# State-space layer of a two-layer network: C products two ring places back, halos on ScalarE, another layout of a chunk's side work

## The chip, the cores and the metric

One Trainium2 chip, of which the program uses one core. The metric is device time in microseconds, the median over runs; less is better.

## The reference

A network of two layers over 2048 rows of 512 features: attention and a mixture of experts, then a selective state space (Mamba) layer and a permuted MLP, each behind a layer norm. The change is in the state-space layer, for which the reference reads, cut to what matters:

```python
proj = hidden_states @ W_in.T
u, gate = jnp.split(proj, 2, axis=-1)                 # 1024 channels each
x = conv_general_dilated(transpose(u), conv_w, padding=[(K - 1, 0)], feature_group_count=D)   # K = 4 taps
u = silu(transpose(x) + conv_b)
dt, Bm, Cm = split(u @ Wx.T, [R, R + N])              # R = 32, N = 16; each then rms-normed
delta = softplus(dt @ Wdt.T + dt_bias)
def step(state, xs):
    d_t, B_t, C_t, u_t = xs
    state = exp(d_t[..., None] * A) * state + (d_t * u_t)[..., None] * B_t[:, None, :]
    return state, einsum('bdn,bn->bd', state, C_t)
y = (scan(step) + u * D_param) * silu(gate)
return y @ W_out.T
```

## The kernel before

The stage works on 8 chunks (c) of 256 time steps. In a chunk there are 8 tiles of 128 channels (t) and, for each, 4 groups of states (gr), so 32 units (q), numbered Q over the whole stage. A unit is a tile of 128 partitions x 4 parts (j) x 256 steps, held in `scan`, a ring of 8 places. What is done to a unit:

- the drive: `spread` multiplies the repeated delta*u (`rep`) by the B rows (`bc`), on GpSimd for even units and on VectorE for odd ones, into `drive`;
- the decays: ScalarE's `decays` writes exp(delta*A) into PSUM, four passes a unit, through three half-unit banks;
- the scan: VectorE's `unit` does four TENSOR_TENSOR_SCANs in place, and after each second unit copies the last states into `state` (the carry);
- the C product: GpSimd multiplies the scanned states by the C rows, into `read`;
- the sum: TensorE's `sum_states` adds over states, two units later (`LAG`); at the end of a channel tile the skip product, and then VectorE's `gate_y`.

`drive` and `read` are the same memory: a part has 257 columns, `drive` is columns 1 to 256 and `read` columns 0 to 255. The C product is thus written in place one column to the left, and the last column keeps the state for the carry. `bc` begins two elements (`PHASE`) off the alignment of the other tiles.

Between the units every engine does side work for the next chunk (and the output of the chunk before), at places that tables of numbers give: on TensorE `AT` says before which unit stand the projection of u (`proj`, 4 pairs of channel tiles), the convolution (`conv`), the rows of B, C and dt (`rows`, `square`, `rms`), the step sizes (`step`), the gate's projection (`gate`) and the output product (`out`) of the chunk before. On ScalarE `U_COPY`, `CONV_OUT`, `SILU`, `ROWS_OUT`, `RMS`, `GATE_OUT`, `STEP_OUT`, `GATE_SILU`, `H_OUT` (`modulate`) and `OUT_COPY` say before which unit's decays their copies and functions stand, on VectorE `NORMED` (`rms_norm`), `DELTA` (`step_sizes`) and two tables for the halos. Each of TensorE's side products takes one of two PSUM banks in turn (`PLACE`), and waits until the product two before it has been read out. The engines' queues are in order, so a late item holds up all behind it.

The halo is the last three columns of u's projection, which the convolution of the next chunk needs: VectorE copies them from `halo` into `upre` and from `upre` into `halo`, a TENSOR_REDUCE of 6 elements each, for each of the 4 pairs of a chunk.

Of the kernel before, what the change touches and what calls it, by code (L numbers as in the profile page):

```python
# [2100 lines left out]
```

## Time and profile before

| | |
|---|---|
| median of 3 runs | 1946.83 us (1944.97 to 1953.23) |
| profiled execution, its own time | 1953.82 us |
| its span, first to last instruction | 1952.0 us |
| busy in the span: TensorE, VectorE, ScalarE, GpSimd | 1620.1, 1375.3, 1094.4, 966.5 us |
| mean granted TensorE clock | 0.829 of full speed |
| state-space stage, first scan to last | 865.7 to 1825.4 us |

The busy times are over the whole program. The part that the change touches is the state-space stage, in which VectorE, GpSimd and TensorE all have much to do, and what counts there is who waits for whom, unit by unit.

### The profile page before, as it was taken

The numbers are of one execution on the slowest core, as the hardware profiler recorded it, in microseconds if no ns is written. First come the engines' busy times: TensorE is split into PE (matmuls) and PEld (weight loads), VectorE is DVE, ScalarE is ACT, GpSimd is POOL, SyncE is SP. The second block draws the span as 40 slices with busy tenths as digits, with TensorE's granted clock in tenths as the row PEclk, the third lists the DMA queues.
The fourth block names the chain that finished last, engine by engine and source line by source line (L and its number), as shares of the span: only waits on it lengthen the run. The fifth ranks groups of instructions, "written<-read, shape, count | busy, mean of one in ns | idle before, by whom it ended". The sixth has DMA issues, their size and how long they took to land. (4 is left out here: it accounts for less than half of the span.)

```text
span 1952.0 us, 24260 instructions
## 1 busy us (share of the span) xinstructions
PE 1620.1 (83%) x8168; PEld 866.7 (44%) x8168; DVE 1375.3 (70%) x2292; ACT 1094.4 (56%) x2026; POOL 966.5 (50%) x598
## 2 busy tenths in 40 slices
PE   6888999999879995778688797987979879745558
PEld 2522222222147443555366474664746647423322
DVE  3257888888064215037998899989999889999423
ACT  2333666667712013257766767668676676765227
POOL 0000000001033203437998898888988888999403
PEclk9765999999965796778699796997969979767678
DMA  5311000000083446633543445434454344645022
GB/s 225 153 53 55 3 3 3 3 3 3 6 279 147 155 135 237 215 88 80 121 112 93 103 112 126 109 92 103 117 123 108 92 104 101 133 98 124 17 92 87
DMA packets 152988, 195.78 MB, mean 100 GB/s; under 512 B 17907, under 2 KB 123139, under 8 KB 151198
## 3 DMA queue, kind: packets, MB, share of 16 engines
q1 hardware_dynamic: 143692, 167.19, 33.0%
q0 software_dynamic: 4608, 16.80, 2.4%
q10 hardware_dynamic: 4564, 10.24, 1.4%
q8 instruction: 65, 1.06, 0.2%
q14 instruction: 59, 0.48, 0.1%
HBM read 141.81 MB, written 52.37 MB: 99 GB/s over the span
## 5 line engine op out<-in xcount | busy, mean ns | idle before, releaser
L1811 DVE TENSOR_TENSOR_SCAN ssm_scan<-ssm_psum,ssm_state,ssm_scan 128x256 f32<-128x256 f32 x1024 | 680.0, 728 | 59.6 <-ACT ssm_psum L1698 59.6
L1430 POOL TENSOR_TENSOR ssm_scan<-ssm_scan,ssm_bc 128x1024 f32<-128x1024 f32 x256 | 557.4, 2181 | 117.7 <-DVE ssm_scan L1811 117.4
L1698 ACT ACTIVATE ssm_psum<-ssm_rep,ssm_a 128x256 f32<-128x256 f32 x1024 | 435.6, 467 | 193.4 <-DVE ssm_scan L1811 191.2
L641 ACT ACTIVATE att_probs<-att_psum 128x1024 f32<-128x1024 f32 x256 | 248.5, 1021 | 108.4 <-PE att_psum L577 108.2
L678 DVE TENSOR_REDUCE att_rowmax<-att_psum 128x1 f32<-128x512 f32 x448 | 278.1, 682 | 42.0 <-PE att_psum L559 42.0
L1534 PE MATMUL ssm_psum<-ssm_scan,ssm_select 128*32 128x256 f32 x2048 | 190.9, 459 | 98.7 <-POOL ssm_scan L1430 98.4
L1410 POOL TENSOR_TENSOR ssm_scan<-ssm_rep,ssm_bc 128x1024 f32<-128x1024 f32 x128 | 255.7, 1998 | 9.5 <-DMA ssm_rep<-drive_rows 9.5
L530 POOL COPY att_v<-v_tokens 128x128 f32<-128x128 f32 x8 | 2.3, 295 | 332.2 <-ACT att_out L635 332.2
L559 PE MATMUL att_psum<-att_k,att_q 72*128 72x512 bf16 x448 | 160.6, 399 | 3.7 <-DVE att_rowmax L678 2.2
L1796 DVE TENSOR_TENSOR ssm_scan<-ssm_rep,ssm_psum 128x1024 f32<-128x1024 f32 x128 | 156.1, 1220 | 1.4 <-DMA ssm_rep<-drive_rows 1.4
L1512 PE MATMUL ssm_psum<-ssm_h,late_weights 128*128 128x256 f32 x512 | 134.0, 421 | 18.2 <-DVE ssm_delta L1785 15.1
L588 PE MATMUL att_psum<-att_probs,att_v 128*32 128x512 f32 x1024 | 139.0, 615 | 0.6 <-ACT att_probs L641 0.6
L1534 PEld LDWEIGHTS ssm_psum<-ssm_scan,ssm_select 128*32 128x32 f32 x2048 | 47.0, 118 | 200.2 <-POOL ssm_scan L1430 109.7
L1478 PE MATMUL ssm_psum<-ssm_upre,late_weights 128*128 128x256 f32 x512 | 132.0, 416 | 3.5 <-ACT late_turned L1611 3.5
L577 PE MATMUL att_psum<-att_q,att_k 74*128 74x512 bf16 x448 | 132.2, 379 | 0.7 <-ACT att_probs L641 0.2
L1468 PE MATMUL ssm_psum<-ssm_h,late_weights 128*128 128x256 f32 x512 | 122.7, 395 | 7.9 <-ACT ssm_h L1593 7.0
L1512 PEld LDWEIGHTS ssm_psum<-ssm_h,late_weights 128*128 128x128 f32 x512 | 105.8, 212 | 50.5 <-DVE ssm_delta L1785 21.2
L1520 PE MATMUL ssm_psum<-ssm_gate,late_weights 128*128 128x256 f32 x512 | 121.0, 391 | 0.6 <-issue 0.6
L1478 PEld LDWEIGHTS ssm_psum<-ssm_upre,late_weights 128*128 128x128 f32 x512 | 104.2, 208 | 33.0 <-ACT late_turned L1611 6.7
L1505 PE MATMUL ssm_psum<-ssm_normed,ssm_wdt 32*128 32x256 f32 x128 | 63.8, 648 | 64.4 <-DVE ssm_delta L1785 32.3
L1468 PEld LDWEIGHTS ssm_psum<-ssm_h,late_weights 128*128 128x128 f32 x512 | 98.9, 197 | 30.7 <-issue 14.7
L1520 PEld LDWEIGHTS ssm_psum<-ssm_gate,late_weights 128*128 128x128 f32 x512 | 98.7, 196 | 20.5 <-issue 6.6
(232 smaller groups left out, 1894.0 us busy)
## 6 DMA issues: line engine op xcount, KB each, us to landing
ssm_rep<-drive_rows SPq DMA_DIRECT2D x256, 256.0 KB, 4.8
qkv_wmod<-in_wmod SPq DMA_DIRECT2D x8, 1536.0 KB, 12.0
late_weights<-in_we SPq DMA_DIRECT2D x8, 1024.0 KB, 14.4
ssm_bc<-bc_rows SPq DMA_DIRECT2D x32, 256.0 KB, 5.0
drive_rows<-ssm_delta SPq DMA_DIRECT2D x64, 128.0 KB
drive_rows<-ssm_du SPq DMA_DIRECT2D x64, 128.0 KB
sorted_rows<-moe_zeros SPq DMA_DIRECT2D x1, 5888.0 KB, 19.2
moe_sorted<-sorted_rows SPq DMA_DIRECT2D x23, 256.0 KB, 3.5
```

Of the source, the lines that this page charges most:

```text
L559: nc.tensor.matmul(ps_m[n % MB], q[0:QROWS, tile[m // QC]], k[0:QROWS, chunk[m % QC]], start=True, stop=True).then_inc(max_scored, 1)
L641: nc.scalar.activation(probs[:, u % RING, :].rearrange("p (j t) -> p j t", j=2), ps_s[u % 2], ACT.Exp).then_inc(exp_done, 1)
L678: nc.vector.tensor_reduce(rowmax[:, m:m + 1], ps_m[n % MB], AX.X, ALU.max).then_inc(max_done, 1)
L1410: nc.gpsimd.tensor_tensor(drive[:, Q % RING], rep[:, s % 2, 1], bc[:, c % 2, 0, gr, :].unsqueeze(1).to_broadcast([P, J, SW]), ALU.mult).th ...
L1430: nc.gpsimd.tensor_tensor(read[:, Q % RING], drive[:, Q % RING], bc[:, c % 2, 1, gr, :].unsqueeze(1).to_broadcast([P, J, SW]), ALU.mult).t ...
L1468: last = nc.tensor.matmul(halves("proj", c, pair)[:, i], win[:, k, m:m + P], h[:, c % 2, k, :], start=(k == 0), stop=(k == KT - 1))
L1478: last = nc.tensor.matmul(halves("conv", c, pair)[:, i], conv[:, 2 * pair + i, k, :], upre[:, pair % 2, i, k:k + SW], start=(k == 0), stop ...
L1512: last = nc.tensor.matmul(halves("gate", c, pair)[:, i], win[:, k, m:m + P], h[:, c % 2, k, :], start=(k == 0), stop=(k == KT - 1))
L1520: nc.tensor.matmul(bank("out", c, m)[:, 0:SW], wout[:, t, m * P:(m + 1) * P], gate[:, c % 2, t, :], start=(t == 0), stop=False)
L1534: last = nc.tensor.matmul(ps_y[t % 2][32 * j:32 * j + 32, :], select[:], read[:, Q % RING, j, :], start=(gr == 0), stop=False)
L1698: nc.scalar.activation(ps_decay[n % HALF_BANKS][:, i], rep[:, s % 2, 0, j, :], ACT.Exp, scale=amat[:, t, gr, j:j + 1]).then_inc(decay_done, 1)
L1811: nc.vector.tensor_tensor_scan(drive[:, Q % RING, j, :], ps_decay[(2 * Q + j // 2) % HALF_BANKS][:, j % 2], drive[:, Q % RING, j, :], stat ...
```

## The change

`scan` loses its extra column. `drive(Q)` is place Q of the ring, and `read(Q)` is place Q - 2: the C product no longer overwrites its own input but the place of the unit two before, whose carry has been taken by then. A place is used again six units after the C product was written there, so the spreads wait for a later sum. `halo` gets two copies, one for each parity of chunk, and ScalarE fills and reads it in `copy_u`; VectorE's two halo functions and their semaphores go. The tables get other numbers, `AT` holds lists, and `modulate` moves from unit 24 to unit 12.

```diff
-        halo = sb("ssm_halo", [P, DT, TAPS - 1])
+        halo = sb("ssm_halo", [P, 2, DT, TAPS - 1])
-        scan = sb("ssm_scan", [P, RING, J, SW + 1])
-        drive, read = scan[:, :, :, 1:], scan[:, :, :, 0:SW]
+        scan = sb("ssm_scan", [P, RING, J, SW])
...
-              9: ("conv", 3), 10: ("out", 0), 11: ("out", 1), 12: ("out", 2), 13: ("rows", 0), 14: ("out", 3), 15: ("square", 0),
+              10: [("conv", 3), ("out", 0)],
+              12: [("out", 1)],
+              14: [("rows", 0)],
+              17: [("square", 0), ("out", 2)],
...
-        SILU, ROWS_OUT, RMS, GATE_SILU, H_OUT = 13, 16, 18, 31, 24
+        SILU, ROWS_OUT, RMS, GATE_SILU, H_OUT = 15, 17, 19, 31, 12
...
-        OUT_COPY = {12: 0, 13: 1, 14: 2, 16: 3}
+        OUT_COPY = {14: 0, 18: 1, 19: 2, 21: 3}
+        def drive(Q):
+            return scan[:, Q % RING]
+        def read(Q):
+            return scan[:, (Q - 2) % RING]
...
-                if Q >= RING:
-                    pool.wait_ge(sum_done, Q - RING + 1)
-                    pool.wait_ge(carry_done, (Q - RING) // 2 + 1)
-                nc.gpsimd.tensor_tensor(drive[:, Q % RING], rep[:, s % 2, 1],
+                if Q >= RING - 2:
+                    pool.wait_ge(sum_done, Q - RING + 3)
+                    if Q >= RING:
+                        pool.wait_ge(carry_done, (Q - RING) // 2 + 1)
+                nc.gpsimd.tensor_tensor(drive(Q), rep[:, s % 2, 1],
...
                     pool.wait_ge(scan_done, (Q + 1) * J)
-                    nc.gpsimd.tensor_tensor(read[:, Q % RING], drive[:, Q % RING],
+                    if Q >= 2:
+                        pool.wait_ge(carry_done, Q // 2)
+                        pool.wait_ge(read_done, Q - 1)
+                    nc.gpsimd.tensor_tensor(read(Q), drive(Q),
...
-                    act.wait_ge(halo_saved, n - 1)
+                if n >= DP:
+                    act.wait_ge(upre_out, n - DP + 1)
+                pair_of = slice(2 * pair, 2 * pair + 2)
+                nc.scalar.copy(upre[:, pair % 2, :, 0:TAPS - 1], halo[:, c % 2, pair_of, :])
+                nc.scalar.copy(halo[:, (c + 1) % 2, pair_of, :], halves("proj", c, pair)[:, :, SW - TAPS + 1:])
                 nc.scalar.copy(upre[:, pair % 2, :, TAPS - 1:], halves("proj", c, pair)).then_inc(upre_out, 1)
...
-                if Q >= RING:
-                    dve.wait_ge(sum_done, Q - RING + 1)
+                if Q >= RING - 2:
+                    dve.wait_ge(sum_done, Q - RING + 3)
```

ScalarE around the silu of u (the two ACT_TABLE_LOADs with an ACTIVATE of 128x2048 between them), before, units 11 to 14 of a chunk; `ssm_psum<-ssm_rep,ssm_a` x4 are the decays of one unit, `ssm_xout` an output copy:

```order
L1611 ACTIVATE late_turned<-ssm_psum,ssm_convb 128x256 x2
L1678 COPY ssm_xout<-ssm_psum 128x256
L1698 ACTIVATE ssm_psum<-ssm_rep,ssm_a 128x256 x4
L1615 ACT_TABLE_LOAD
L1615 ACTIVATE late_turned<-late_turned 128x2048
L1588 ACT_TABLE_LOAD
L1678 COPY ssm_xout<-ssm_psum 128x256
L1698 ACTIVATE ssm_psum<-ssm_rep,ssm_a 128x256 x4
L1678 COPY ssm_xout<-ssm_psum 128x256
L1698 ACTIVATE ssm_psum<-ssm_rep,ssm_a 128x256 x8
```

and with the change, from `modulate` (128x256 x4 into `ssm_h`) before unit 12 to unit 16:

```order
L1617 ACTIVATE ssm_h<-ssm_h,mod 128x256 x4
L1726 ACTIVATE ssm_psum<-ssm_rep,ssm_a 128x256 x4
L1639 ACTIVATE late_turned<-ssm_psum,ssm_convb 128x256 x2
L1726 ACTIVATE ssm_psum<-ssm_rep,ssm_a 128x256 x4
L1706 COPY ssm_xout<-ssm_psum 128x256
L1726 ACTIVATE ssm_psum<-ssm_rep,ssm_a 128x256 x4
L1643 ACT_TABLE_LOAD
L1643 ACTIVATE late_turned<-late_turned 128x2048
L1612 ACT_TABLE_LOAD
L1726 ACTIVATE ssm_psum<-ssm_rep,ssm_a 128x256 x8
```

An output copy stood right ahead of the silu's unit and one right behind the silu; now the one ahead is a unit earlier, behind nothing but a convolution's copy, and `modulate` has come in two units before that.

ScalarE around the first step size of a chunk (`ssm_delta<-ssm_psum,ssm_dtb` is a step's first pass), before:

```order
L1698 ACTIVATE ssm_psum<-ssm_rep,ssm_a 128x256 x20
L1593 ACTIVATE ssm_h<-ssm_h,mod 128x256 x4
L1651 ACTIVATE ssm_delta<-ssm_psum,ssm_dtb 128x256 x2
L1655 ACTIVATE ssm_psum<-ssm_psum,ssm_dtb 128x256 x2
L1657 ACTIVATE ssm_psum<-ssm_psum 128x512
L1659 ACTIVATE ssm_psum<-ssm_psum 128x512
```

and with the change:

```order
L1726 ACTIVATE ssm_psum<-ssm_rep,ssm_a 128x256 x8
L1693 COPY ssm_gate<-ssm_psum 128x512
L1679 ACTIVATE ssm_delta<-ssm_psum,ssm_dtb 128x256 x2
L1683 ACTIVATE ssm_psum<-ssm_psum,ssm_dtb 128x256 x2
L1685 ACTIVATE ssm_psum<-ssm_psum 128x512
L1687 ACTIVATE ssm_psum<-ssm_psum 128x512
L1726 ACTIVATE ssm_psum<-ssm_rep,ssm_a 128x256 x4
```

`modulate` stood between 20 decays and the step; now a gate copy stands there.

TensorE from the first output product (`ssm_gate,late_weights` with `ident,ssm_xres`) on, before; `ssm_wx` is `rows`, `ssm_group` is `square`, `ssm_scan,ssm_select` x4 the sum of one unit, `ssm_skip` the skip product:

```order
L1520 MATMUL ssm_psum<-ssm_gate,late_weights 128x256 x8
L1524 MATMUL ssm_psum<-ident,ssm_xres 128x128 x2
L1534 MATMUL ssm_psum<-ssm_scan,ssm_select 32x256 x4
L1520 MATMUL ssm_psum<-ssm_gate,late_weights 128x256 x8
L1524 MATMUL ssm_psum<-ident,ssm_xres 128x128 x2
L1534 MATMUL ssm_psum<-ssm_scan,ssm_select 32x256 x4
L1520 MATMUL ssm_psum<-ssm_gate,late_weights 128x256 x8
L1524 MATMUL ssm_psum<-ident,ssm_xres 128x128 x2
L1534 MATMUL ssm_psum<-ssm_scan,ssm_select 32x256 x4
L1485 MATMUL ssm_psum<-late_turned,ssm_wx 64x256 x8
L1534 MATMUL ssm_psum<-ssm_scan,ssm_select 32x256 x4
L1539 MATMUL ssm_psum<-late_turned,ssm_skip 128x256
```

and with the change:

```order
L1509 MATMUL ssm_psum<-late_turned,ssm_wx 64x256 x8
L1558 MATMUL ssm_psum<-ssm_scan,ssm_select 32x256 x12
L1515 MATMUL ssm_psum<-ssm_group,ssm_normed 128x3 x2
L1544 MATMUL ssm_psum<-ssm_gate,late_weights 128x256 x8
L1548 MATMUL ssm_psum<-ident,ssm_xres 128x128 x2
L1558 MATMUL ssm_psum<-ssm_scan,ssm_select 32x256 x4
L1563 MATMUL ssm_psum<-late_turned,ssm_skip 128x256
L1521 MATMUL ssm_psum<-ident,ssm_rwide 64x128 x2
L1558 MATMUL ssm_psum<-ssm_scan,ssm_select 32x256 x4
L1544 MATMUL ssm_psum<-ssm_gate,late_weights 128x256 x8
L1548 MATMUL ssm_psum<-ident,ssm_xres 128x128 x2
L1536 MATMUL ssm_psum<-ssm_h,late_weights 128x256 x8
```

Before, three outputs stood ahead of `rows` with one sum between each two, and the fourth right behind; now output 2 comes after `rows`, three sums and `square`, and output 3 is followed at once by a gate product (`ssm_h,late_weights`) with no sum between.

## Rows read from the trace of the kernel before

**Rows 1.** Windows: engines' busy us (x instructions), granted clock, DMA share, GB/s.
```profile
core 0: us, PE busy (x) PEld busy (x) DVE busy (x) ACT busy (x) POOL busy (x), PEclk, DMA share, GB/s
989.00:1598.00 609.00, 521.11 (x2924) 346.50 (x2920) 553.58 (x905) 424.26 (x946) 530.09 (x280) 0.85 0.48 109
1598.00:1716.00 118.00, 98.56 (x568) 64.77 (x568) 110.47 (x182) 83.32 (x187) 104.86 (x56) 0.88 0.48 108
1716.00:1830.00 114.00, 59.44 (x370) 26.73 (x370) 109.04 (x174) 57.57 (x135) 105.59 (x55) 0.60 0.41 93
```

**Rows 2.** Timeline of VectorE: silu of u in chunk 0; unit 31 of chunks 0, 5, 6, 7.
```profile
921.05 1.39 DVE L1811 TENSOR_TENSOR_SCAN ssm_scan<-ssm_psum,ssm_state,ssm_scan 128x256 f32<-128x256 f32 x2 [1.19 <-ACT ssm_psum L1698]
...
988.82 1.39 DVE L1811 TENSOR_TENSOR_SCAN ssm_scan<-ssm_psum,ssm_state,ssm_scan 128x256 f32<-128x256 f32 x2 [2.88 <-ACT ssm_psum L1698]
...
1598.17 1.39 DVE L1811 TENSOR_TENSOR_SCAN ssm_scan<-ssm_psum,ssm_state,ssm_scan 128x256 f32<-128x256 f32 x2 [3.11 <-ACT ssm_psum L1698]
...
1715.82 1.39 DVE L1811 TENSOR_TENSOR_SCAN ssm_scan<-ssm_psum,ssm_state,ssm_scan 128x256 f32<-128x256 f32 x2 [1.47 <-ACT ssm_psum L1698]
...
1822.73 2.66 DVE L1811 TENSOR_TENSOR_SCAN ssm_scan<-ssm_psum,ssm_state,ssm_scan 128x256 f32<-128x256 f32 x4
```

**Rows 3.** Groups by line, 840 to 1860 us: busy, mean ns, idle before.
```profile
L1811 DVE TENSOR_TENSOR_SCAN ssm_scan<-ssm_psum,ssm_state,ssm_scan 128x256 f32<-128x256 f32 x1024 | 680.0, 728 | 59.6 <-ACT ssm_psum L1698 59.6
...
L1430 POOL TENSOR_TENSOR ssm_scan<-ssm_scan,ssm_bc 128x1024 f32<-128x1024 f32 x256 | 557.4, 2181 | 117.7 <-DVE ssm_scan L1811 117.4
...
L1410 POOL TENSOR_TENSOR ssm_scan<-ssm_rep,ssm_bc 128x1024 f32<-128x1024 f32 x128 | 255.7, 1998 | 9.5 <-DMA ssm_rep<-drive_rows 9.5
...
L1823 DVE TENSOR_TENSOR ssm_gate<-ssm_psum,ssm_gate 128x256 f32<-128x256 f32 x64 | 25.9, 405 | 11.1 <-PE ssm_psum L1539 11.1
...
L1678 ACT COPY ssm_xout<-ssm_psum 128x256 f32<-128x256 f32 x32 | 11.9, 372 | 73.1 <-PE ssm_psum L1524 73.0
...
L1773 DVE TENSOR_REDUCE ssm_halo<-ssm_upre 128x6 f32<-128x6 f32 x28 | 4.2, 151 | 0.3 <-DVE ssm_upre L1767 0.3
```

**Rows 4.** Timeline of VectorE, chunk 4: start, length, idle before.
```profile
1404.86 2.67 DVE L1811 TENSOR_TENSOR_SCAN ssm_scan<-ssm_psum,ssm_state,ssm_scan 128x256 f32<-128x256 f32 x4 [3.38 <-ACT ssm_psum L1698]
...
1416.98 5.24 DVE L1811 TENSOR_TENSOR_SCAN ssm_scan<-ssm_psum,ssm_state,ssm_scan 128x256 f32<-128x256 f32 x8 [0.81 <-ACT ssm_psum L1698]
...
1426.79 0.42 DVE L1823 TENSOR_TENSOR ssm_gate<-ssm_psum,ssm_gate 128x256 f32<-128x256 f32 x1 [0.62 <-PE ssm_psum L1539]
...
1445.10 0.69 DVE L1785 TENSOR_TENSOR ssm_delta<-ssm_delta,ssm_psum 128x512 f32<-128x512 f32 x1 [1.36 <-ACT ssm_psum L1659]
```

**Rows 5.** Timeline of ScalarE, chunk 4, units 12, 18 and 24.
```profile
1397.11 0.37 ACT L1678 COPY ssm_xout<-ssm_psum 128x256 f32<-128x256 f32 x1 [2.09 <-PE ssm_psum L1524]
1397.37 1.67 ACT L1698 ACTIVATE ssm_psum<-ssm_rep,ssm_a 128x256 f32<-128x256 f32 x4
1399.06 1.28 ACT L1615 ACT_TABLE_LOAD   x1
...
1403.58 0.37 ACT L1678 COPY ssm_xout<-ssm_psum 128x256 f32<-128x256 f32 x1
...
1421.81 0.50 ACT L1639 ACTIVATE ssm_rwide<-ssm_rms 128x64 f32<-128x64 f32 x3
...
1440.21 2.07 ACT L1593 ACTIVATE ssm_h<-ssm_h,mod 128x256 f32<-128x256 f32 x4
```

**Rows 6.** Timeline of TensorE, chunk 4, around units 2 and 28.
```profile
1363.19 0.64 PE L1534 MATMUL ssm_psum<-ssm_scan,ssm_select 128*32 128x256 f32 x8 [2.91 <-POOL ssm_scan L1430]
1363.76 5.41 PE L1478 MATMUL ssm_psum<-ssm_upre,late_weights 128*128 128x256 f32 x16
...
1369.67 3.72 PE L1468 MATMUL ssm_psum<-ssm_h,late_weights 128*128 128x256 f32 x16
...
1436.22 1.08 PE L1534 MATMUL ssm_psum<-ssm_scan,ssm_select 128*32 128x256 f32 x8
...
1457.63 6.25 PE L1512 MATMUL ssm_psum<-ssm_h,late_weights 128*128 128x256 f32 x16 [2.15 <-DVE ssm_delta L1785]
...
1464.38 3.72 PE L1512 MATMUL ssm_psum<-ssm_h,late_weights 128*128 128x256 f32 x16
```

**Rows 7.** Groups of GpSimd: the fold of the gate into the output weights.
```profile
L1416 POOL TENSOR_TENSOR late_weights<-late_weights,ssm_xout 128x512 f32<-128x512 f32 x8 | 9.9, 1276 | 0.0
```

More of the change, by code:

```diff
@@ L1255, in state_space @@
         xdst = scratch.x3.rearrange("(k p) t -> p k t", p=P)
-        AT = {0: ("proj", 0), 1: ("proj", 1), 3: ("conv", 0), 4: ("proj", 2), 5: ("conv", 1), 6: ("proj", 3), 7: ("conv", 2),
-              9: ("conv", 3), 10: ("out", 0), 11: ("out", 1), 12: ("out", 2), 13: ("rows", 0), 14: ("out", 3), 15: ("square", 0),
-              16: ("gate", 0), 17: ("gate", 1), 19: ("rms", 0), 21: ("step", 0), 22: ("step", 1),
-              24: ("step", 2), 25: ("step", 3), 27: ("gate", 2), 28: ("gate", 3)}
+        AT = {0: [("proj", 0), ("proj", 1)],
+              3: [("conv", 0)],
+              4: [("proj", 2)],
+              6: [("conv", 1)],
+              7: [("proj", 3)],
+              9: [("conv", 2)],
+              10: [("conv", 3), ("out", 0)],
+              12: [("out", 1)],
+              14: [("rows", 0)],
+              17: [("square", 0), ("out", 2)],
+              18: [("rms", 0)],
+              19: [("out", 3), ("gate", 0)],
+              20: [("step", 0)],
+              22: [("step", 1), ("gate", 1)],
+              23: [("step", 2)],
+              26: [("gate", 2)],
+              28: [("step", 3), ("gate", 3)]}
         AHEAD = {"proj": 1, "conv": 1, "gate": 1, "rows": 1, "square": 1, "rms": 1, "step": 1, "out": -1}
@@ L1266, in state_space @@
         LATE = {0: ("gate", 2), 1: ("step", 2), 2: ("gate", 3), 3: ("step", 3)}
+        STEP_AHEAD = (1, 1, 1, 1)
         def at(c, q):
@@ L1273, in at @@
             if q in AT:
-                kind, i = AT[q]
-                if 0 <= c + AHEAD[kind] < SCH:
-                    found.append((kind, c + AHEAD[kind], i))
+                for kind, i in AT[q]:
+                    of = c + (STEP_AHEAD[i] if kind == "step" else AHEAD[kind])
+                    if 0 <= of < SCH:
+                        found.append((kind, of, i))
             return found
@@ L1533, in sum_states @@
                 for j in range(J):
-                    last = nc.tensor.matmul(ps_y[t % 2][32 * j:32 * j + 32, :], select[:], read[:, Q % RING, j, :],
+                    last = nc.tensor.matmul(ps_y[t % 2][32 * j:32 * j + 32, :], select[:], read(Q)[:, j, :],
                                             start=(gr == 0), stop=False)
@@ L1825, in _ @@
             dve.wait_ge(zeroed, 2)
-            for pair in range(DP):
-                carry_halo(0, pair)
-                save_halo(0, pair)
             dve.wait_ge(weights_in, 16 * 8)
```

46 lines of the change are left out of this document (14 added, 32 removed).

## The prediction

> **What bounds the kernel now.** The state-space stage is about half of the span, so I read it chunk by chunk in the windows [rows 1]: over chunks 1 to 5 VectorE is busy 553.58 of 609 us, 110.7 a chunk, and idle 11.1. GpSimd (530.09, 106.0 a chunk) and TensorE (521.11, 104.2) are close behind. The last chunk has no side work; from its predecessor's last unit to its own it is 1822.73 - 1715.82 = 106.9 us [rows 2], 3.34 a unit, the floor as the scan is written. The steady period is (1598.17 - 988.82) / 5 = 121.9 [rows 2]. So 3.8 us a chunk is VectorE's side work and 11.1 is waiting.
>
> Whom it waits for is in [rows 3]: the scans for ScalarE's decays 59.6 us, the gating product for TensorE's sums 11.1. Where, is in [rows 4], chunk 4: 3.38 at unit 13, 0.81 at unit 16, 0.62 for a sum at 19, 1.36 for a step size at 24; and about 3 more at unit 31 (2.88 and 3.11 in [rows 2]). Why, is on ScalarE [rows 5]. Its decays have three half banks, so it can be at most 1.5 units ahead. Before the silu of u it waits 2.09 us for output product 0; then table load, silu and table load take 1403.58 - 1399.06 = 4.5 us, and another output copy stands before the decays of unit 13. At unit 24 the 2.07 us of `modulate` stand ahead of a step size. Two places show a silu with less in front of it [rows 2]: 1.19 us in chunk 0, which has no output copies, and 1.47 at the end of chunk 6, which has no `modulate`.
>
> **The change, part by part.** (a) *Order on ScalarE.* `modulate` goes to unit 12, and units 13 and 14 hold one small copy each. ScalarE needs 1.67 us a unit for decays [rows 5] against VectorE's 3.34, so it is 1.5 units ahead again by unit 14. The silu of u moves to unit 15; output 0 was multiplied at unit 10, so nothing is waited for, and the other output copies come after it. I price each silu at the undisturbed 1.2 us (ends: 0.7, if ScalarE starts it as early as the banks allow, and 1.5): 2.4 a chunk for two. Step sizes now stand at 23, 24, 27, 29. A step takes ScalarE about 2.8 us (its four passes stand between the end of `modulate`, two microseconds after 1440.21, and the delta at 1445.10 [rows 4, 5]). From unit 23: gate copy 0.5, step 2.8, decays 1.7, step 2.8. VectorE comes to the first delta with 0.9 to spare and to the second just as it is ready: 0.3 (ends 0 and 1.4, the wait now). Steps 2 and 3 stand behind units in which ScalarE recovers.
>
> The table switches bear on the silu's floor. The Trainium skill ("ScalarE: Activation LUTs", what a table load costs) adds a drain of about 1.38 us to each load of 1283 ns. By that the block of 4.5 us would be 7.2, each of 14 silus would cost 2.7 us more, 38 in all, and a fifth of the gain would be left. The trace shows no such drain behind the loads, so the rows decide.
>
> (b) *Order on TensorE.* Outputs 2 and 3 go from units 12 and 14 to 17 and 19, so four output products and `rows` no longer stand nearly back to back, which made the sum 0.62 late [rows 4]. New waits take their place: `rows` (unit 14) waits for the silu, 3 to 5 us of idle TensorE; `square` (17) needs the bank that output copy 1 gives back at ScalarE's unit 18; and `rms_norm` stands at unit 19, not 21. From the silu's end: `rows` 3.7, its copies 0.7, decays, the copy of output 1 and `square` 3.7, output 2 about 4.2, a sum and `rms` 1.8: 14.1 us. VectorE reaches `rms_norm` 14.0 after the silu. I take a wait of 0.5, with ends 0 and 2: after 2.91 us of idle TensorE the next 16 products took 5.41 us where 3.72 is usual [rows 6], and that may befall `rows`.
>
> (c) *The ring.* C products are written two places back, so a place is free only six units after its use, not eight: a spread of unit Q needs sum Q-6. The tightest is the spread of unit 23, which needs sum 17, queued behind output 3 and gate 0 (7.9 us at full clock). By the same walk it ends some 2 us before: no cost. With 6.25 us for 16 products, as at half clock [rows 6], it is 3 to 4 us late. The new waits of the C product, on the carry and on itself, cost nothing: both precede the scan for which GpSimd waits anyway.
>
> (d) *GpSimd's durations.* The C product takes 2181 ns, the B spread 1998 [rows 3]. Both multiply 1024 elements by the same bc tile, two elements off alignment. The spread's other input is aligned; the C product reads and writes the scan tile in runs of 257-element step. Without the column it has the spread's pattern, so I take 1998: 256 x 0.18 = 47 us less on GpSimd, none on the path, since the scans wait for ScalarE alone [rows 3]. Ends: 2181, and 2.55 us, twice the 1276 ns of a 512-element product whose three operands start alike [rows 7]. VectorE's scans already start at four different offsets in a unit, and four take 2.67 us everywhere [rows 4]; I expect no change there.
>
> (e) *Halos.* VectorE loses 2 x 28 reduces of 0.15 us [rows 3], which overlap their neighbours and cost some 0.11 each: 0.9 us a chunk. ScalarE gets two small copies before each of its `copy_u`. It has no such row; bounds are 0.17 us, a third of three passes of 32 elements or fewer [rows 5], and nothing. At most 8 x 0.17 = 1.4 us a chunk, in units 2, 3, 6 and 10, where ScalarE waits for VectorE. Before the first unit they are partly on the path: +0.7.
>
> **Sum.** A steady chunk keeps 2.4 + 0.3 + 0.5 of waits and 0.5 of gaps too small for a row, 3.7 instead of 11.1; with the halos -8.3, over five chunks -41.5. Chunk 0 keeps its late gate and step work in units 0 to 5; of 1.19, 1.4 and 2.88 later it keeps 3, and halos: -3.3. Chunk 6 has 118 - 110.5 = 7.5 us idle [rows 1]: to 3.7, and halos, -4.7. The start +0.7. Together -48.8 us. The profiled execution took 1953.82, so about 1905; it was 7 us above the median of the three runs, 1946.83, and against that I say 1898.
>
> **Rivals.** *A: TensorE's chain.* A chunk falls to about 113 us while TensorE needs 104 of it at a granted 0.85 [rows 1]. If the wait at unit 14 drops its clock to the lower level until gate 0, output 2 and sum 17 come 3 to 4 us late each and most of the 8 us is given back: 1918 to 1940. For it: 5.41 and 6.25 behind waits of 2 to 3 us. Against: the next block stood at 3.72 each time [rows 6]. Chance 0.16.
>
> *B: GpSimd becomes the bound.* With C products of 2.55 us four units cost it 4 x 2.51 + 2 x 1.96 + 0.7 = 14.7 against VectorE's 13.4, 117 a chunk, the last one too: about 1930. The crossing is near 2.23 us. Chance 0.05. The Trainium skill ("GPSIMD Engine Reference", instruction dispatch) gives 2.5 cycles an element as the floor of a two-input pass; an estimate from it is 2133 ns for 1024 elements, so a C product of 1998 could not be. The spread's row stands below that floor already.
>
> *C: slower.* The same loss of clock, lasting through most of a chunk. At the lower level twelve 16-product blocks are 75 us, four outputs 28, forty sums and skips at 1.08 or more 44 [rows 6], the rest about 18: 165 a chunk against 96 at full clock. TensorE passes 122, the present period, once more than 0.37 of its work runs at the lower level; at 0.42 it stands at 124 to 125, seven chunks of +2.5: 1964. Granted 0.85 over chunks 1 to 5 says that most of it now runs at full clock. Chance 0.06.
>
> *D: the waits only move,* to units 15 and 24, and the halos alone remain, -6: 1941. The two undisturbed silus speak against it. Chance 0.08.
>
> **The numbers.** My forecast has 0.65 and its own range 1880 to 1916 (low: silus at 0.7, nothing at the others; high: every upper end). The range 1880 to 1932 takes in B and most of A and leaves out under 2 in 10. A measurement of this kernel tells about 0.5% from no change. Faster: forecast, B, nearly all of A, 0.86; same: most of D and the edges of A and C, 0.08; slower: C, 0.06.
>
> **What would show it.** The steady period falls to about 113.5 us. Waits for decays of some 1.2 us are left at units 15 and 31, none at 16. The C product's row reads about 2.0 us; ScalarE's wait for output products, 73 us [rows 3], shrinks to the one at the end. I am wrong if VectorE waits before a spread (the ring) or over 2 us at `rms_norm`, or if the granted clock falls below 0.8 in the middle chunks.

## Result and profile after

The changed kernel takes 1887.59 us, the median of 4 runs (1879.21 to 1893.53), against 1948.01 for the kernel before in 4 runs: a ratio of 0.968, 95% interval [0.964, 0.973]. Its profiled execution took 1893.53 us (span 1891.7, granted clock 0.856), 60.3 less than that of before.

Windows of the changed kernel over the stretch of [rows 1], 5.4 of its chunks:

```profile
989.00:1598.00 609.00, 532.99 (x3162) 375.33 (x3166) 588.72 (x932) 458.97 (x1055) 540.99 (x303) 0.92 0.51 117
```

VectorE is busy 588.72 of the 609 us where it was busy 553.58, and idle 3.8 us a chunk instead of 11.1. TensorE's granted clock rose from 0.85 to 0.92.

VectorE's timeline has the first scan, and the last carry of chunks 0, 1, 2, 5, 6 and 7 (the copy of last states behind unit 31).

```profile
859.48 0.75 DVE L1824 TENSOR_TENSOR_SCAN ssm_scan<-ssm_psum,ssm_state,ssm_scan 128x256 f32<-128x256 f32 x1 [0.86 <-ACT ssm_psum L1726]
...
977.93 0.17 DVE L1829 TENSOR_REDUCE ssm_state<-ssm_scan 128x8 f32<-128x8 f32 x1
...
1092.68 0.17 DVE L1829 TENSOR_REDUCE ssm_state<-ssm_scan 128x8 f32<-128x8 f32 x1
...
1205.50 0.17 DVE L1829 TENSOR_REDUCE ssm_state<-ssm_scan 128x8 f32<-128x8 f32 x1
...
1543.92 0.17 DVE L1829 TENSOR_REDUCE ssm_state<-ssm_scan 128x8 f32<-128x8 f32 x1
...
1656.73 0.17 DVE L1829 TENSOR_REDUCE ssm_state<-ssm_scan 128x8 f32<-128x8 f32 x1
...
1763.98 0.17 DVE L1829 TENSOR_REDUCE ssm_state<-ssm_scan 128x8 f32<-128x8 f32 x1
```

The distance between carries is the period: (1543.92 - 1205.50) / 3 = 112.81 us, with 114.75 for chunk 1 and 112.81 for chunk 6. The sum by stage, before to after:

| stretch | before | after | change | predicted |
|---|---|---|---|---|
| ahead of the stage, to the first scan | 865.67 | 859.48 | -6.2 | +0.7 |
| chunk 0 | 125.86 | 118.45 | -7.4 | -3.3 |
| chunks 1 to 5 | 609.4 | 566.0 | -43.4 | -41.5 |
| chunk 6 | 117.65 | 112.81 | -4.8 | -4.7 |
| chunk 7 | 106.90 | 107.25 | +0.4 | 0 |

The waits that are left, in chunk 4, are two for decays (units 15 and 31) and one at `rms_norm`. The fourth row is `rms_norm` in chunk 1.

```profile
1370.05 2.67 DVE L1824 TENSOR_TENSOR_SCAN ssm_scan<-ssm_psum,ssm_state,ssm_scan 128x256 f32<-128x256 f32 x4 [0.90 <-ACT ssm_psum L1726]
...
1384.85 0.47 DVE L1792 SCALAR_TENSOR_TENSOR ssm_normed<-ssm_proj,ssm_lnw,ssm_psum 64x256 f32<-64x256 f32 x1 [1.67 <-PE ssm_psum L1521]
...
1428.41 2.68 DVE L1824 TENSOR_TENSOR_SCAN ssm_scan<-ssm_psum,ssm_state,ssm_scan 128x256 f32<-128x256 f32 x4 [0.34 <-ACT ssm_psum L1726]
...
1046.42 0.47 DVE L1792 SCALAR_TENSOR_TENSOR ssm_normed<-ssm_proj,ssm_lnw,ssm_psum 64x256 f32<-64x256 f32 x1 [3.26 <-PE ssm_psum L1521]
```

There is no wait longer than 0.3 us before a spread, a sum's gating product or a step size in a steady chunk. The groups by line that answer to [rows 3]:

```profile
L1824 DVE TENSOR_TENSOR_SCAN ssm_scan<-ssm_psum,ssm_state,ssm_scan 128x256 f32<-128x256 f32 x1024 | 676.7, 728 | 13.6 <-ACT ssm_psum L1726 13.6
L1455 POOL TENSOR_TENSOR ssm_scan<-ssm_scan,ssm_bc 128x1024 f32<-128x1024 f32 x256 | 510.9, 1997 | 94.3 <-DVE ssm_scan L1824 92.9 <-PE ssm_psum L1558 1.2
...
L1432 POOL TENSOR_TENSOR ssm_scan<-ssm_rep,ssm_bc 128x1024 f32<-128x1024 f32 x128 | 255.5, 1996 | 22.8 <-PE ssm_psum L1558 13.4 <-DMA ssm_rep<-drive_rows 9.4
...
L1706 ACT COPY ssm_xout<-ssm_psum 128x256 f32<-128x256 f32 x32 | 11.8, 368 | 58.9 <-PE ssm_psum L1548 58.9
L1628 ACT COPY ssm_upre<-ssm_halo 128x6 f32<-128x6 f32 x28 | 5.1, 181 | 3.7 <-PE ssm_psum L1493 3.7
L1629 ACT COPY ssm_halo<-ssm_psum 128x6 f32<-128x6 f32 x28 | 4.3, 153 | 0.0
```

The scans wait 13.6 us for decays instead of 59.6. The C product takes 1997 ns, and GpSimd has a new wait of 13.4 us for sums before its spreads: that is the shorter ring. ScalarE still waits 58.9 us for output products: in chunk 4, 3.50 us before output copy 2 and 1.65 before copy 3. The silu of u on ScalarE in chunk 4, with its first table load and the decays behind its second:

```profile
1364.52 1.28 ACT L1643 ACT_TABLE_LOAD   x1
...
1369.04 3.31 ACT L1726 ACTIVATE ssm_psum<-ssm_rep,ssm_a 128x256 f32<-128x256 f32 x8
```

From the first load to the next decays it is 4.52 us, the same as from the first load to the output copy before. The Trainium skill ("ScalarE: Activation LUTs", what a table load costs) adds a drain of about 1.38 us to each load, by which an estimate for the block is 7.2 us; the trace contradicts that drain here too.

### The profile page after: what moved, and what is told of

It is laid out like the page before. It is cut to its first block and busy times, and to the rows that moved or that the text cites. A ratio compares the mean times of both kernels' runs of the same rounds, so it can differ in the third digit from the quotient of the medians.

```text
span 1891.7 us, 24451 instructions
## 1 busy us (share of the span) xinstructions
PE 1578.7 (83%) x8168; PEld 864.5 (46%) x8168; DVE 1367.6 (72%) x2228; ACT 1100.9 (58%) x2090; POOL 921.0 (49%) x598
## 5 line engine op out<-in xcount | busy, mean ns | idle before, releaser
L1824 DVE TENSOR_TENSOR_SCAN ssm_scan<-ssm_psum,ssm_state,ssm_scan 128x256 f32<-128x256 f32 x1024 | 676.7, 728 | 13.6 <-ACT ssm_psum L1726 13.6
L1455 POOL TENSOR_TENSOR ssm_scan<-ssm_scan,ssm_bc 128x1024 f32<-128x1024 f32 x256 | 510.9, 1997 | 94.3 <-DVE ssm_scan L1824 92.9
L1432 POOL TENSOR_TENSOR ssm_scan<-ssm_rep,ssm_bc 128x1024 f32<-128x1024 f32 x128 | 255.5, 1996 | 22.8 <-PE ssm_psum L1558 13.4
L1558 PE MATMUL ssm_psum<-ssm_scan,ssm_select 128*32 128x256 f32 x2048 | 164.2, 422 | 93.6 <-POOL ssm_scan L1455 93.6
L1536 PE MATMUL ssm_psum<-ssm_h,late_weights 128*128 128x256 f32 x512 | 136.9, 428 | 20.1 <-DVE ssm_delta L1798 15.8
L1544 PE MATMUL ssm_psum<-ssm_gate,late_weights 128*128 128x256 f32 x512 | 134.6, 422 | 1.8 <-ACT late_turned L1639 1.3
L1493 PE MATMUL ssm_psum<-ssm_h,late_weights 128*128 128x256 f32 x512 | 128.5, 410 | 8.6 <-ACT ssm_h L1617 3.7
L1502 PE MATMUL ssm_psum<-ssm_upre,late_weights 128*128 128x256 f32 x512 | 124.6, 398 | 10.5 <-ACT late_turned L1639 10.5
L1536 PEld LDWEIGHTS ssm_psum<-ssm_h,late_weights 128*128 128x128 f32 x512 | 108.3, 217 | 46.4 <-DVE ssm_delta L1798 18.6
L1493 PEld LDWEIGHTS ssm_psum<-ssm_h,late_weights 128*128 128x128 f32 x512 | 103.8, 207 | 35.2 <-issue 13.9
L1544 PEld LDWEIGHTS ssm_psum<-ssm_gate,late_weights 128*128 128x128 f32 x512 | 107.1, 213 | 26.3 <-issue 7.0
L1502 PEld LDWEIGHTS ssm_psum<-ssm_upre,late_weights 128*128 128x128 f32 x512 | 99.9, 198 | 33.6 <-ACT late_turned L1639 13.3
L559 PEld LDWEIGHTS att_psum<-att_k,att_q 72*128 72x128 bf16 x448 | 35.5, 98 | 135.4 <-DVE att_rowmax L678 93.9
```

Source lines behind the costliest of these rows:

```text
L559: nc.tensor.matmul(ps_m[n % MB], q[0:QROWS, tile[m // QC]], k[0:QROWS, chunk[m % QC]], start=True, stop=True).then_inc(max_scored, 1)
L1432: nc.gpsimd.tensor_tensor(drive(Q), rep[:, s % 2, 1], bc[:, c % 2, 0, gr, :].unsqueeze(1).to_broadcast([P, J, SW]), ALU.mult).then_inc(poo ...
L1455: nc.gpsimd.tensor_tensor(read(Q), drive(Q), bc[:, c % 2, 1, gr, :].unsqueeze(1).to_broadcast([P, J, SW]), ALU.mult).then_inc(read_done, 1)
L1493: last = nc.tensor.matmul(halves("proj", c, pair)[:, i], win[:, k, m:m + P], h[:, c % 2, k, :], start=(k == 0), stop=(k == KT - 1))
L1502: last = nc.tensor.matmul(halves("conv", c, pair)[:, i], conv[:, 2 * pair + i, k, :], upre[:, pair % 2, i, k:k + SW], start=(k == 0), stop ...
L1536: last = nc.tensor.matmul(halves("gate", c, pair)[:, i], win[:, k, m:m + P], h[:, c % 2, k, :], start=(k == 0), stop=(k == KT - 1))
```

## The experiments

**The parts one by one.** Four kernels: the kernel before with only the new ring, only ScalarE's halos, only the new tables; and the changed kernel with the old ring. The edit of the first, cut to two places, and in reverse that of the fourth:

```diff
-        scan = sb("ssm_scan", [P, RING, J, SW + 1])
+        scan = sb("ssm_scan", [P, RING, J, SW])
...
-                    nc.gpsimd.tensor_tensor(read[:, Q % RING], drive[:, Q % RING],
+                    if Q >= 2:
+                        pool.wait_ge(carry_done, Q // 2)
+                        pool.wait_ge(read_done, Q - 1)
+                    nc.gpsimd.tensor_tensor(read(Q), drive(Q),
```

> The kernel before with the ring edit alone: no extra column, C products two places back, old tables, halos on VectorE. Theory (order of side work is what pays): GpSimd's C product falls from 2181 to about 1998 ns, and the period of a steady chunk stays at 121.9 us within 0.5, so the time stays within 0.3% of 1948. Rival 1 (GpSimd's lateness had a share in the waits): the period falls by 1 us or more, the time by 8 or more. Rival 2 (the ring of six bites where four output products make the sums late): VectorE waits at its spread, the period rises by 0.5 or more.

> The kernel before with the halo edit alone (two small copies of ScalarE in place of two reduces of VectorE, and the wait for the zeroed tiles that now stands ahead of ScalarE's big weight load). Theory: the period falls by 0.9 us a chunk to 121.0, and the first load of h lands some 3 us earlier because the weight load is issued behind it: together -8 to -10 us. Rival: ScalarE's 1.2 us more a chunk come out as longer waits ahead of the silus, period 121.9 or more, time within 3 us of before.

> The kernel before with the new tables alone: TensorE's, ScalarE's and VectorE's side work placed as in the change, the column and the in-place C product kept, halos still on VectorE at places that fit the new order. Theory: nearly the whole gain, period 113.7 us (112.8 plus 0.9 for the halos), time about 1896. Rival (the parts need each other, since GpSimd with C products of 2181 ns is busy 105.5 of 112.8): period 115 or more, time above 1905.

> The changed kernel with the extra column and the in-place C product back: C product 2181 ns, ring of eight. Theory: GpSimd's 47 us were hidden, the period stays 112.8 and the time within 3 us of the changed kernel's 1888; GpSimd's waits for sums (13 us) go. Rival 1: GpSimd is near its bound and the time rises by 7 us or more. Rival 2: the ring of six cost something, and the time falls.

| kernel | median us (runs) | ratio to before | mean of chunks 1 to 5, us | first scan to last carry, us | C product ns |
|---|---|---|---|---|---|
| before | 1948.35 (19) | | 121.9 | 959.8 | 2181 |
| ring alone | 1942.82 (10) | 0.997 [0.994, 1.001] | 121.5 | 959.9 | 2000 |
| halos alone | 1942.50 (10) | 0.997 [0.995, 1.000] | 121.3 | 959.0 | 2179 |
| tables alone | 1904.51 (4) | 0.978 [0.972, 0.984] | 114.5 | 911.6 | 2182 |
| changed, old ring | 1878.27 (4) | 0.966 [0.959, 0.973] | 112.6 | 902.0 | 2180 |
| changed | 1887.59 (4) | 0.968 [0.964, 0.973] | 113.2 | 904.5 | 1997 |

From chunk 2 on both changed kernels have a steady period of 112.8 us.

GpSimd's groups by line, ring alone and then the changed kernel with the old ring:

```profile
L1441 POOL TENSOR_TENSOR ssm_scan<-ssm_scan,ssm_bc 128x1024 f32<-128x1024 f32 x256 | 511.9, 2000 | 160.4 <-DVE ssm_scan L1822 159.9
```

```profile
L1444 POOL TENSOR_TENSOR ssm_scan<-ssm_scan,ssm_bc 128x1024 f32<-128x1024 f32 x256 | 557.1, 2180 | 60.9 <-DVE ssm_scan L1813 60.3
L1424 POOL TENSOR_TENSOR ssm_scan<-ssm_rep,ssm_bc 128x1024 f32<-128x1024 f32 x128 | 255.6, 1997 | 9.1 <-DMA ssm_rep<-drive_rows 9.1
```

The ring makes each C product 0.18 us shorter, and GpSimd then waits nearly that much longer for scans: 160 us where it waited 117 in [rows 3]. The path gets nothing: the stage takes 959.9 us where it took 959.8. With the old ring GpSimd's wait for sums is gone and the steady period is the same to 0.01 us, so the shorter ring costs nothing either. The 2.5 us by which the two changed kernels' stages differ are in chunk 1, where `rms_norm` waited 3.26 us with the new ring and 0.42 with the old. "The placements" below shows where such a wait comes from.

The tables bring 7.4 us a chunk. That is 0.8 less than was expected, and the time, 1904.51 us, came between the theory's 1896 and the rival's 1905. The halos bring 0.6 us a chunk alone; over the stage only 0.7 us of that is left, because chunk 6 takes 119.1 us instead of 117.6. The 8 to 10 us that were expected of them were not reached, though the interval of the 5.9 measured takes them in. On top of the tables the halos bring 1.3 us a chunk with the new ring and 1.8 with the old (114.5 to 113.2 and 112.6). VectorE's busy time over these chunks says how that splits: 110.8 us a chunk before, 110.1 with the tables, and 109.4 with both, in either ring; idle 11.1, 4.4, and then 3.8 with the new ring and 3.3 with the old. So the halos bring 0.7 us of work less. The idle time differs by the waits at `rms_norm`: over chunks 1 to 5 they add up to 12.8 us with the tables alone, where they change between 1.6 and 3.2, to 9.9 in the changed kernel and to 7.1 in the one with the old ring. Whether the halos have a part in that is open.

**The placements.** Three kernels are the changed one with one number altered: `modulate` back at unit 24, output copy 1 at unit 16, or `bc` aligned like the other tiles.

```diff
-        SILU, ROWS_OUT, RMS, GATE_SILU, H_OUT = 15, 17, 19, 31, 12
+        SILU, ROWS_OUT, RMS, GATE_SILU, H_OUT = 15, 17, 19, 31, 24
```

```diff
-        OUT_COPY = {14: 0, 18: 1, 19: 2, 21: 3}
+        OUT_COPY = {14: 0, 16: 1, 19: 2, 21: 3}
```

```diff
-    PHASE = 2
+    PHASE = 0
```

> The changed kernel with modulate back before unit 24 (one number). Theory: it stands between two step sizes again; the delta of pair 1 at unit 24 is about 2 us late and the silu at unit 31 comes later too, period +2 to +3 us, time +12 to +20 (about 1900 to 1908). Rival (ScalarE's place for it does not matter once the output copies are away from the silu): period +0.5 at most.

> The changed kernel with the copy of output product 1 before unit 16 instead of 18 (one number), so that TensorE's square product gets its bank as soon as the rows have been copied. Theory (the wait of 1.67 us at rms_norm comes from that bank: TensorE waits 3.7 us for this copy ahead of square in each chunk): the wait goes, period 111.2, time 10 to 12 us less, about 1877. Rival (the wait comes from output 2, which is simply 4 us of work ahead of rms): the wait shrinks by less than 0.5, time within 3 us of the changed kernel.

> The changed kernel with the bc tile aligned like the others (its two-element offset taken away). Theory (GpSimd's pace on two SBUF inputs depends on how their starts stand to each other; equal starts cost what the 512-element product shows, 1276 ns): C product and spread go to about 2.4 to 2.55 us, four units cost GpSimd 6 x 2.4 + 0.7 = 15 us or more against VectorE's 13.4, it becomes the bound, and the period is 120 or more, time 1945 or more. Rival (the offset of the written tile made 2181 out of 1998, the inputs' do nothing): both stay at 2.0 and the time does not move.

| kernel | median us (runs) | ratio to before | period us (`PHASE` 0: mean of chunks 1 to 5) |
|---|---|---|---|
| `modulate` at 24 | 1901.30 (4) | 0.975 [0.972, 0.979] | 116.0 |
| copy 1 at 16 | 1870.98 (6) | 0.961 [0.957, 0.964] | 111.03 |
| `PHASE` 0 | 1915.18 (4) | 0.983 [0.979, 0.986] | 117.1 |

*Copy at 16.* `rms_norm` waits for TensorE's `rms`, and so for what stands ahead of that. TensorE in chunk 4 of the changed kernel, from `rows` to `rms`:

```profile
1367.87 3.64 PE L1509 MATMUL ssm_psum<-late_turned,ssm_wx 128*64 128x256 f32 x16 [1.65 <-ACT late_turned L1643]
...
1376.65 0.60 PE L1515 MATMUL ssm_psum<-ssm_group,ssm_normed 64*128 64x3 f32 x4 [3.71 <-ACT ssm_xout L1706]
1377.18 5.41 PE L1544 MATMUL ssm_psum<-ssm_gate,late_weights 128*128 128x256 f32 x16
...
1384.16 0.65 PE L1521 MATMUL ssm_psum<-ident,ssm_rwide 128*64 128x128 f32 x4
```

and the same stretch with the copy at unit 16:

```profile
1358.64 3.64 PE L1509 MATMUL ssm_psum<-late_turned,ssm_wx 128*64 128x256 f32 x16 [1.64 <-ACT late_turned L1643]
...
1364.05 0.57 PE L1515 MATMUL ssm_psum<-ssm_group,ssm_normed 64*128 64x3 f32 x4 [0.34 <-ACT ssm_proj L1655]
1364.55 3.72 PE L1544 MATMUL ssm_psum<-ssm_gate,late_weights 128*128 128x256 f32 x16
...
1370.48 0.62 PE L1521 MATMUL ssm_psum<-ident,ssm_rwide 128*64 128x128 f32 x4 [0.57 <-ACT ssm_rwide L1667]
```

`square` waited 3.71 us for the bank that output copy 1 reads; now 0.34, for its own input. And the output product behind it takes 3.72 us again instead of 5.41. Windows over the output product say why, first the changed kernel and then copy 1 at 16 (the clock is the third number from the right):

```profile
1376.00:1383.00 7.00, 6.35 (x28) 5.29 (x30) 6.96 (x12) 3.02 (x10) 6.43 (x5) 0.76 0.13 24
```

```profile
1364.00:1372.00 8.00, 7.38 (x48) 5.47 (x49) 7.96 (x13) 5.01 (x15) 7.43 (x4) 1.00 0.46 85
```

After 3.71 us of idle TensorE the granted clock of the stretch is 0.76, so part of it ran at the lower of the two levels, 1.2 GHz; behind the short wait it is 1.00, 2.4 GHz throughout. VectorE's wait at `rms_norm` is gone, and the period falls by 1.78 us, the 1.67 of that wait and 0.1. ScalarE's wait for output products falls from 58.9 to 25.1 us, about what its four copies behind the last chunk wait.

*`modulate` at 24.* VectorE's timeline in chunk 4, at `rms_norm` and at the second step size:

```profile
1392.78 0.47 DVE L1792 SCALAR_TENSOR_TENSOR ssm_normed<-ssm_proj,ssm_lnw,ssm_psum 64x256 f32<-64x256 f32 x1 [3.09 <-PE ssm_psum L1521]
...
1412.03 0.69 DVE L1798 TENSOR_TENSOR ssm_delta<-ssm_delta,ssm_psum 128x512 f32<-128x512 f32 x1 [1.70 <-ACT ssm_psum L1687]
```

The step size waits 1.70 us, for `modulate` stands ahead of it. The silus' waits are 0.91 and 0.34, as without the edit, so moving `modulate` away from unit 12 gives the silu nothing, and the later silu at unit 31 that was expected did not come. The other 1.42 us of the 3.2 come at `rms_norm`, and their window and rows on TensorE are:

```profile
1382.00:1392.00 10.00, 8.85 (x34) 6.88 (x34) 7.65 (x12) 4.52 (x14) 9.43 (x6) 0.66 0.21 48
```

```profile
1383.15 1.01 PE L1515 MATMUL ssm_psum<-ssm_group,ssm_normed 64*128 64x3 f32 x4 [3.71 <-ACT ssm_xout L1706]
1384.09 6.43 PE L1544 MATMUL ssm_psum<-ssm_gate,late_weights 128*128 128x256 f32 x16
```

The wait for the bank is again 3.71 us, but the clock behind it is 0.66 and the output product takes 6.43. One and the same wait is followed by a block of 5.41 or of 6.43 us. What differs ahead of it is that `rows` waited 3.28 us here and 1.65 there, but that does not decide it. Chunk 1 of the changed kernel is shown first, then chunk 1 of a kernel that differs from it only ahead of the stage (with two lines swapped, see "The start of the stage"). `rows` waited as long in both, and `square` waited 3.71 us for the bank in both:

```profile
1027.84 3.64 PE L1509 MATMUL ssm_psum<-late_turned,ssm_wx 128*64 128x256 f32 x16 [2.96 <-ACT late_turned L1643]
...
1037.56 6.60 PE L1544 MATMUL ssm_psum<-ssm_gate,late_weights 128*128 128x256 f32 x16
```

```profile
1029.29 3.64 PE L1509 MATMUL ssm_psum<-late_turned,ssm_wx 128*64 128x256 f32 x16 [2.97 <-ACT late_turned L1643]
...
1038.79 5.17 PE L1544 MATMUL ssm_psum<-ssm_gate,late_weights 128*128 128x256 f32 x16
```

The granted clock over the two output products is 0.56 and 0.71, and `rms_norm` waits 3.26 and 1.61 us. What sets the length is open.

Chunk 6 of the kernel with `modulate` at 24 shows what the clock alone is worth. There `rows` ran slowly, 5.32 us, and the bank wait shrank to 2.02, since it ends with the same output copy; the output product then ran at a clock of 1.00, and VectorE reached `rms_norm` without a wait:

```profile
1616.45 3.72 PE L1544 MATMUL ssm_psum<-ssm_gate,late_weights 128*128 128x256 f32 x16
```

```profile
1622.43 0.47 DVE L1792 SCALAR_TENSOR_TENSOR ssm_normed<-ssm_proj,ssm_lnw,ssm_psum 64x256 f32<-64x256 f32 x1
```

The chunk before it, with 6.44 us for the product, waited 3.10. In chunk 2 of the changed kernel `rows` took 5.33 us as well, with a bank wait of 2.02 and 5.41 for the product: the slow `rows` cost nothing, the slow product its 1.67.

*`PHASE` 0.* VectorE's scans and GpSimd's C product and spread, by line:

```profile
L1824 DVE TENSOR_TENSOR_SCAN ssm_scan<-ssm_psum,ssm_state,ssm_scan 128x256 f32<-128x256 f32 x1024 | 677.0, 728 | 35.0 <-POOL ssm_scan L1432 22.8 <-ACT ssm_psum L1726 11.0
L1455 POOL TENSOR_TENSOR ssm_scan<-ssm_scan,ssm_bc 128x1024 f32<-128x1024 f32 x256 | 599.9, 2373 | 8.2 <-DVE ssm_scan L1824 8.2
...
L1432 POOL TENSOR_TENSOR ssm_scan<-ssm_rep,ssm_bc 128x1024 f32<-128x1024 f32 x128 | 304.1, 2376 | 10.8 <-DMA ssm_rep<-drive_rows 9.2 <-PE ssm_psum L1558 1.6
```

All three operands start alike and the pass takes 2.37 us. Now the scans wait for GpSimd's spreads, 22.8 us, and GpSimd for nearly nothing: it is the bound, as in rival B. Four units take it 14.6 us, and eight times that is 116.8, nearly the chunk's 117.1. The last chunk, which has no side work, goes from 107.3 to 113.8 us. The theory had the direction and the engine right and the size too large: 120 us or more a chunk and 1945 or more in all were expected.

**The start of the stage.** The first scan came 6.2 us earlier, which no step foresaw. Only 1.6 of it is there when SyncE issues the first load of `ssm_h`. In the trace of before, and then of after, the rows around that load are (a `q` behind an engine's name is its DMA queue):

```profile
792.94 0.36 SPq L1307 DMA_DIRECT2D ssm_h<-x_layer_normalised  x1
...
792.95 0.46 ACTq L1701 DMA_DIRECT2D late_weights<-in_win  x1
...
799.81 2.07 ACT L1593 ACTIVATE ssm_h<-ssm_h,mod 128x256 f32<-128x256 f32 x4 [5.09 <-DMA ssm_h<-x_layer_normalised]
```

```profile
791.37 0.36 SPq L1328 DMA_DIRECT2D ssm_h<-x_layer_normalised  x1
...
791.67 0.39 ACTq L1730 DMA_DIRECT2D late_weights<-in_win  x1
...
794.97 2.07 ACT L1617 ACTIVATE ssm_h<-ssm_h,mod 128x256 f32<-128x256 f32 x4 [1.59 <-DMA ssm_h<-x_layer_normalised]
```

`modulate` starts 6.87 us after the load's issue before, 3.60 after. ScalarE's own transfer, 2 MB of weights, was issued at the same time as the load; now it comes 0.3 us behind it. The reason is a line of the change, `act.wait_ge(zeroed, 2)`, that the diff ahead of the prediction left out: ScalarE now reads `halo`, and so waits until GpSimd has zeroed it, and the wait stands ahead of its first transfer in this stage. Two kernels tell that apart from the rest: the changed one with the two lines swapped, and the kernel before with the wait added.

```diff
+            act.dma_start(win[:, :, DI:], d["win"].rearrange("(k p) m -> p k m", p=P)[:, :, DI:]).then_inc(g.win_in[1], 16)
             act.wait_ge(zeroed, 2)
-            act.dma_start(win[:, :, DI:], d["win"].rearrange("(k p) m -> p k m", p=P)[:, :, DI:]).then_inc(g.win_in[1], 16)
```

```diff
+            act.wait_ge(zeroed, 2)
             act.dma_start(win[:, :, DI:], d["win"].rearrange("(k p) m -> p k m", p=P)[:, :, DI:]).then_inc(g.win_in[1], 16)
```

> The changed kernel with ScalarE's 2 MB weight load issued before the wait for the zeroed tiles, as in the kernel before. Theory: the load goes out together with the first load of h, whose data then land 3 us later (modulate starts 8 us and not 3.6 us after SP issues it), and the stage starts 3 us later. Rival: the earlier start of the stage in the changed kernel's profile was chance, and nothing moves there.

> The kernel before with one wait more: ScalarE issues the 2 MB of in_win's other half after it has seen the zeroed buffers, as the changed kernel does, some 0.3 us after SyncE has issued the first load of ssm_h, and not at the same time. Theory of the load order: the first modulate of the stage starts 3.6 us after SyncE's issue instead of 6.9, ScalarE's wait ahead of it is 1.6 us instead of 5.1, and the chunks are as before (period 121.9). Rival: the halo work on ScalarE or the ring in the changed kernel is what moved it; then 6.9 us stays.

One run each: 1891.56 us with the lines swapped and 1942.56 for before with the wait. A difference of 3 us is below what one run can tell, so the traces decide, the swapped one first:

```profile
789.32 0.36 SPq L1328 DMA_DIRECT2D ssm_h<-x_layer_normalised  x1
...
789.32 0.46 ACTq L1729 DMA_DIRECT2D late_weights<-in_win  x1
...
796.24 2.07 ACT L1617 ACTIVATE ssm_h<-ssm_h,mod 128x256 f32<-128x256 f32 x4 [5.15 <-DMA ssm_h<-x_layer_normalised]
```

```profile
784.95 0.36 SPq L1307 DMA_DIRECT2D ssm_h<-x_layer_normalised  x1
...
785.24 0.39 ACTq L1702 DMA_DIRECT2D late_weights<-in_win  x1
...
788.45 2.07 ACT L1593 ACTIVATE ssm_h<-ssm_h,mod 128x256 f32<-128x256 f32 x4 [1.51 <-DMA ssm_h<-x_layer_normalised]
```

Swapped, it is 6.92 us (8 was expected); with the wait added to the kernel before, 3.50. It holds in all thirteen traces: four without the wait ahead of the transfer have 6.81 to 6.97 us, nine with it 3.50 to 3.64. From the issue to the first scan it is 71.2 to 72.7 us (mean 71.7) against 67.4 to 69.4 (mean 68.3), so the 3.3 us are kept. The last 1.3 of the 6.2 lies between `modulate` and the first scan, 65.86 us before and 64.52 after, and is within the spread of the thirteen traces, 63.8 to 65.9. No price for the halo copies at the start can be seen: 68.57 in the kernel without them, 67.4 to 69.4 with.

**The best version.** These are two kernels with output copy 1 at unit 16, one with the old ring and one with the new, measured on one chip.

> The changed kernel with both edits that did no harm or some good by themselves: output copy 1 of ScalarE at unit 16 instead of 18, and the ring of before (extra column, C product in place, eight deep). Theory: VectorE bounds the chunks of the state space, the ring lies on GpSimd alone, so the period is that of the copy at 16 with the new ring, 111.0 us, while the C product is back at 2.18 us and GpSimd's waits for sums are gone; the median is then within 4 us of the other kernel of this call. Rival: the old ring was truly faster by itself (1878.3 against 1887.6 in the two calls) because VectorE or TensorE pays for the ring somewhere; then the median is 6 to 10 us below the other's, and the period or the first chunk shorter.

> The changed kernel with output copy 1 at unit 16 once more, beside the same with the ring of before, on one chip. Theory: 1871 us again, period 111.0 us, within 4 us of the one with the old ring. Rival (the new ring costs something): 6 to 10 us above it.

With the old ring 1871.27 us (6 runs, 0.960 [0.957, 0.963]), with the new one 1875.73 (6 runs, 0.962 [0.959, 0.965]); the same kernel took 1870.98 in the table above. The periods are 111.05 and 111.04, and from first scan to last carry it is 892.3 and 892.4 us. The 4.5 us between the two are a little over the 4 expected, but the stage is equal, so they are not the ring's. The medians 1878.27 and 1887.59 above differ by 9 us, and of the 16.7 between their profiled executions 10.7 lie ahead of the stage (first scan at 848.81 and 859.48 us), 2.5 in the wait of chunk 1, and 3.6 behind the stage. Why the parts outside the stage differ is not shown. By their medians the versions with copy 1 at 16 are 0.6% to 0.9% faster than the changed kernel, and their stage is 12 us shorter, 892.4 against 904.5.

## Why the prediction was right

1898 us was predicted, with a range of 1880 to 1932, and 1887.59 measured. Of its steps:

- *(a) ScalarE's order.* Right in place: VectorE waits for decays at units 15 and 31 and not at 16. The two silus were priced at 2.4 us and cost 0.90 + 0.34 = 1.24; the lower end, "0.7, if ScalarE starts it as early as the banks allow", was the better guide. The step sizes were priced at 0.3 and cost nothing. `modulate` at 24 shows what they would have cost: 1.70. One sign did not come: ScalarE's wait for output products was to shrink from 73 us to the one at the end, and it is 58.9. It moved to copies 2 and 3, where VectorE does not feel it; with copy 1 at 16 it is 25.1.
- *(b) TensorE's order.* The chain was the right one and its size off: 0.5 predicted, 1.67 measured in a steady chunk and 3.26 in chunk 1, which is over the 2 us that the prediction named as a sign of being wrong. The step that failed is "after 2.91 us of idle TensorE the next 16 products took 5.41 us where 3.72 is usual, and that may befall `rows`": it befell the output product behind `square`, priced at full clock. 5.41 - 3.72 = 1.69 is the whole wait, as chunk 6 of `modulate` at 24 shows, where the product took 3.72 behind the same output copy and the wait was nothing. The rest of the walk was off on both sides by nearly the same: `rms` would have ended 15.4 us after the silu, not 14.1 (17.1 less 1.7), and VectorE came after 15.4, not 14.0. That is rival A in small, behind another wait: 1.7 us a chunk instead of most of 8.
- *(c) The ring.* No cost, right, but the walk picked the wrong place. VectorE's spread of unit 23, called the tightest, does not wait. GpSimd's of unit 26 does, 1.1 to 2.7 us in chunks 0 to 5: it needs sum 20, which stands behind gate product 1, and in chunk 4 that took 6.62 us for 16 products. It is GpSimd's spare time; VectorE waits 0.3 us for sums in the whole stage. The two kernels with the old ring show the same steady periods.
- *(d) GpSimd's durations.* 1998 ns predicted, 1997 measured; 47 us less on GpSimd, none on the path, shown from both sides. The crossing near 2.23 us was bracketed, not measured: at 2.37 us for C product and spread GpSimd is the bound, with a period of 117.1, and at 2.18 with 2.00 for the spread it is not. By the floor of about 2.5 cycles an element in the Trainium skill ("GPSIMD Engine Reference", instruction dispatch), an estimate for the pass is 2133 ns at the least; 256 C products at 1997 stand below it.
- *(e) Halos.* 0.9 us a chunk predicted, 0.7 of work measured. The 1.3 to 1.8 in all with the new tables holds waits at `rms_norm` that differ from kernel to kernel. The copies on ScalarE cost 181 and 153 ns each, near the bound of 0.17, in units where ScalarE waits for VectorE anyway. At the start +0.7 was predicted; nothing of that can be seen, and -3.3 came from the order of two transfers, a line whose effect on a queue was not walked through.
- *The sum.* A steady chunk keeps 0.90 + 1.67 + 0.34 = 2.91 us in rows and 0.55 in gaps, 3.46, where 3.7 was predicted. That it comes so near is in part luck: 1.5 us less for silus and steps, 1.2 more for `rms_norm`. The rest of the way from 113.5 to 112.8 is VectorE's own work, 109.4 us a chunk where 109.8 was reckoned. Chunk 0 gave 7.4 instead of 3.3: in VectorE's timeline its late waits fell by 4.4, to what the two silus cost elsewhere, its early ones by 1.9, which had been taken as unchanged, and its work by 1.1. Of the 12.7 us between the predicted -48.8 and the -61.5 at the end of the stage, 6.9 are the start's, 4.1 chunk 0's and 1.9 chunks 1 to 5's.
- *The rivals.* C and D did not come, and A only in small. The clock rose to 0.92 while TensorE's busy time fell from 104.2 to 98.7 us a chunk. C's price of 75 us for twelve blocks took 6.25 us as a block at the lower level; the granted clock over those products was 0.59, and in chunk 2 of the kernel with the two lines swapped 16 products took 6.74 at 0.54, so a whole block at the lower level costs more than C reckoned. B needs passes above 2.23 us.
